# Moving one accumulator drain in four from VectorE to a ScalarE copy and an accumulating DMA

## What is computed

```python
h = linear_with_lora(x)                              # (8*128, 512)
q = dequant_matmul(h, qw_q, scales_q)                # 32 heads of 128
k, v = dequant_matmul(h, qw_k, scales_k), dequant_matmul(h, qw_v, scales_v)   # 8 heads of 128
ctx = softmax(mask(rope(q) @ rope(k).T / sqrt(128))) @ v
x = x + dequant_matmul(ctx, qw_o, scales_o)          # scales_o: one row of 512 for each head
x = x + ffn(low_rank(x))
```

## Time and profile before

| | |
|---|---|
| median of 3 runs | 567.71 us (567.18 to 568.55) |
| span of the profiled execution | 567.4 us (its own time isn't given apart from the span) |
| TensorE, matmuls | 544.6 us busy, 3183 instructions |
| VectorE | 485.5 us, 627 |
| ScalarE | 362.8 us, 939 |
| GpSimd | 400.2 us, 410 |
| DMA | 51.93 MB, mean 92 GB/s |

### The profile page before, as it was taken

How to read it: one execution, slowest core, us unless ns; L and a number is a source line. 1 busy time by engine, 2 the same in 40 slices (tenths; PEclk the granted TensorE clock), 3 DMA queues, 4 the chain that set the end, 5 groups by cost and what they waited for, 6 DMA issues and landing times.

```text
span 567.4 us, 10591 instructions
## 1 busy us (share of the span) xinstructions
PE 544.6 (96%) x3183; PEld 431.7 (76%) x3187; DVE 485.5 (86%) x627; ACT 362.8 (64%) x939; POOL 400.2 (71%) x410
## 2 busy tenths in 40 slices
PE   8999989999999999999999999999999999987985
PEld 6654778878888888888888888888888888864432
DVE  2753859998999899979997999799979998976997
ACT  2574476656665766576657665766576657556795
POOL 3005677799679977997799779977997799761053
PEclk9999999999999999999999999999999999999899
DMA  8932526412541254125422542154224312200003
GB/s 297 230 85 56 153 70 168 112 43 63 156 103 49 60 160 99 51 59 153 104 54 55 149 110 55 55 141 118 52 59 129 92 43 69 57 0 2 0 20 129
DMA packets 38173, 51.93 MB, mean 92 GB/s; under 512 B 12101, under 2 KB 20453, under 8 KB 38149
## 3 DMA queue, kind: packets, MB, share of 16 engines
q1 hardware_dynamic: 35652, 46.94, 31.5%
q10 hardware_dynamic: 2016, 3.48, 2.0%
q0 software_dynamic: 480, 1.22, 0.7%
HBM read 28.55 MB, written 2.10 MB: 54 GB/s over the span
## 4 chain that ended last, share of the span: by engine, by line
PE 82%; DVE 9%; issue 2%; ACT 2%; POOL 2%; DMA 2%; SPq 0%; DVEq 0%; ACTq 0%; POOLq 0%
PE pair L1389 23%; PE pair L1390 23%; PE flow L1378 9%; PE flow L1506 9%; PE flow L1498 4%; PE pair L1307 2%; DVE raw_v L1072 1%; PE flow L1383 1%; PE pair L1324 1%; PE flow L1307 1%; DVE y_max L1182 1%; DMA swap_q<-raw_q 1%; DVE ctx_lo L1093 1%; DVE probs L1194 1%; DVE rope_c L1194 1%
## 5 line engine op out<-in xcount | busy, mean ns | idle before, releaser
L1086 DVE SCALAR_TENSOR_TENSOR accT<-pair,so_now,accT 128x1024 f32<-128x1024 f32 x125 | 157.3, 1275 | 13.7 <-PE pair L1390 12.9
L1072 DVE SCALAR_TENSOR_TENSOR raw_q<-pair,sc_now,raw_q 128x1024 f32<-128x1024 f32 x90 | 115.4, 1283 | 6.3 <-ACT raw_q L769 2.9
L562 POOL TENSOR_TENSOR probs<-probs,rowinv 128x512 f32<-128x512 f32 x64 | 66.7, 1043 | 64.7 <-DVE rowinv L1059 64.6
L714 ACT ACTIVATE probs<-flow,negmax 128x128 f32<-128x128 f32 x248 | 87.6, 368 | 32.8 <-DVE negmax L1040 32.8
L1389 PE MATMUL pair<-ctx_hi,wo 128*128 128x512 f32 x256 | 104.9, 410 | 2.7 <-issue 1.5
L1390 PE MATMUL pair<-ctx_lo,wo 128*128 128x512 f32 x256 | 100.3, 392 | 0.0
L1389 PE MATMUL pair<-h_hi,wq 128*128 128x512 f32 x240 | 99.9, 416 | 0.0
L1390 PE MATMUL pair<-h_lo,wq 128*128 128x512 f32 x240 | 94.1, 392 | 0.0
L531 POOL TENSOR_TENSOR rope_s<-swap_q,consts 128x512 f32<-128x512 f32 x62 | 80.2, 1293 | 9.9 <-DMA swap_q<-raw_q 9.9
L543 POOL TENSOR_TENSOR qT<-rope_c,rope_s 128x512 f32<-128x512 f32 x62 | 79.4, 1280 | 4.4
L531 POOL TENSOR_TENSOR rope_c<-raw_q,consts 128x512 f32<-128x512 f32 x62 | 78.8, 1294 | 0.0
(11 more groups left out here) (243 smaller groups left out, 977.7 us busy)
## 6 DMA issues: line engine op xcount, KB each, us to landing
swap_q<-raw_q SPq DMA_DIRECT2D x62, 256.0 KB, 3.7
wq_i<-in_L_attn_qw_q SPq DMA_DIRECT2D x8, 1024.0 KB, 5.9
wo_i<-in_L_attn_qw_o SPq DMA_DIRECT2D x32, 256.0 KB, 2.7
swap_k<-raw_k SPq DMA_DIRECT2D x14, 256.0 KB, 3.6
wkv_i<-in_L_attn_qw_k SPq DMA_DIRECT2D x8, 256.0 KB, 3.6
wkv_i<-in_L_attn_qw_v SPq DMA_DIRECT2D x8, 256.0 KB, 4.0
stage<-in_x ACTq DMA_DIRECT2D x4, 256.0 KB, 4.8
probs<-in_L_ffn_w ACTq DMA_DIRECT2D x4, 256.0 KB, 7.2
```

Of the source, the lines that this page charges most:

```text
L562: pool.tensor_tensor(pr, pr, rowinv[:, f, :].unsqueeze(2).broadcast_to([P, HB, P]), ALU.mult).then_inc(probs_done, 1)
L714: e = act.activation(probs[:, 0, f, seq(b)], bank[:, seq(b)], ACT.Exp, bias=negmax[:, f, b:b + 1], accum_out=rowsum[:, f, b:b + 1])
L1072: dve.scalar_tensor_tensor(out=into, in0=flat(pair[pair_of(h, (kind, j), last, first)][:, :, :]), scalar=sc_now[:, scale_slot(kind, h), j: ...
L1086: dve.scalar_tensor_tensor(out=a, in0=flat(pair[pair_of(h, (O, c), last, first)][:, :, :]), scalar=so_now[:, (h if c == 0 else h - 1) % 2, ...
```

## The change

In heads 0, 1 and 2 of every group, head 0 of the first and head 2 of the last group excepted, step (O, 3) is no longer drained by VectorE. ScalarE copies the pair into a new tile `part_out` [128, 1024], times the scale (`part_output`, at the end of the head). GpSimd issues, in the next head, right behind the copy of `so_now`, a DMA that adds `part_out` onto `accT[:, 3, :]` (`add_part`). There is one `part_out`, so ScalarE's copy waits until the DMA before has landed (semaphore `d_added`). VectorE's next drain of chunk 3 (head 3 of a group, head 2 of the last one) waits for the DMA instead of for its own drain before. The waits that counted drains are recomputed: a pair that held such a step is free when ScalarE has copied it.

```diff
+        part_out = sb("part_out", [P, T])
...
+        d_added, part_made = sem("d_added"), sem("part_made")
...
+        ADDED_BY_DMA = (O, 3)
...
+        def added_by_dma(h, s, last):
+
+            return s == ADDED_BY_DMA and h % REP < REP - 1 and not (last and h >= 2)
+
+        def by_act(h, s, last):
+            return s[0] != O and s[1] == 0 or added_by_dma(h, s, last)
+
+        def dma_adds(g, h):
+
+            return (REP - 1) * g + h
...
+                    def add_part(late):
+
+                        _, c = ADDED_BY_DMA
+                        if not added_by_dma(late, (O, c), last and late >= 0) or first and late <= 0:
+                            return
+                        pool.dma_start(accT[:, c, :], part_out[:, :], accum_op=ALU.add).then_inc(d_added, 16)
...
-                            pool.wait_ge(dve_drained, drains_by(g, h - 1, (O, 3), first, last))
+                            pool.wait_ge(dve_drained, drains_by(g, h - 1, (O, 2), first, last))
+                            if added_by_dma(h - 1, (O, 3), last and h >= 1):
+                                pool.wait_ge(act_drained, drains_by(g, h - 1, (O, 3), first, last))
+                                wait(pool, d_added, 16 * (dma_adds(g, h - 1) - 1))
+                            if h == 1 or not added_by_dma(h - 1, (O, 3), last and h >= 1):
+                                pool.wait_ge(dve_drained, drains_by(g, h - 1 if h != 1 else -1, (O, 3), first, last))
                         pool.tensor_copy(so_now[:, h % 2:h % 2 + 1, :], so_cols[:, bass.ds(n, 1), :]).then_inc(so_set, 1)
+                        add_part(h - 1)
...
+                    def part_output():
+
+                        _, c = ADDED_BY_DMA
+                        if not present(h, (O, c), first, last) or not added_by_dma(h, (O, c), last):
+                            return
+                        act.wait_ge(step_done, steps_by(g, h, (O, c), first, last))
+                        wait(act, d_added, 16 * (dma_adds(g, h) - 1))
+                        wait(act, so_set, n)
+                        act.activation(part_out[:, :], flat(pair[pair_of(h, (O, c), last, first)][:, :, :]), ACT.Copy,
+                                       scale=so_now[:, (h - 1) % 2, c:c + 1]).then_inc(act_drained, 1)
...
                     seed_mask(1)
+                    part_output()
...
-                        if not present(h, (O, c), first, last):
+                        if not present(h, (O, c), first, last) or added_by_dma(h, (O, c), last):
                             return
...
-                        if not (first and (h == 0 or h == 1 and c > 0)):
+                        if added_by_dma(h - 1, (O, c), last and h > 0):
+                            dve.wait_ge(d_added, 16 * dma_adds(g, h - 1))
+                        elif not (first and (h == 0 or h == 1 and c > 0)):
                             dve.wait_ge(dve_drained, drains_by(g, h - 1, (O, c), first, last))
...
-                            pe.wait_ge(dve_drained, drains_by(g, 1, (O, 3), first, last))
+                            pe.wait_ge(act_drained, drains_by(g, 1, (O, 3), first, last))
```

More of the change, by code:

```diff
@@ L242, in present @@
             return not (last and (s[0] in (K, V) or s[0] == Q and h >= 2))
-        def by_act(s):
-            return s[0] != O and s[1] == 0
+        def added_by_dma(h, s, last):
[4 more added lines that the diff above has]
+            return (REP - 1) * g + h
         def pair_of(h, s, last=False, first=False):
@@ L254, in pair_of @@
             return at % 3 if at < len(STEPS) - 1 else 1
-        ACT_GROUP = sum(by_act(s) for _, s in STEPS)
+        ACT_GROUP = sum(by_act(h, s, False) for h, s in STEPS)
         DVE_GROUP = len(STEPS) - ACT_GROUP
@@ L266, in drains_by @@
         def drains_by(g, h, s, first, last):
-            act = by_act(s)
+            act = by_act(h, s, last and h >= 0)
+            skipped = sum(by_act(0, (O, c), False) == act for c in range(1, C))
+            group = ACT_GROUP if act else DVE_GROUP
             if h < 0:
-                later = [t for t in PERIOD[h][PERIOD[h].index(s) + 1:] if by_act(t) == act]
-                return ACT_GROUP * g - len(later) if act else DVE_GROUP * g - (SKIPPED + len(later))
-            mine = [t for t in STEPS if present(*t, first, last) and by_act(t[1]) == act]
+                later = [t for t in PERIOD[h][PERIOD[h].index(s) + 1:] if by_act(h, t, False) == act]
+                return group * g - (skipped + len(later))
+            mine = [t for t in STEPS if present(*t, first, last) and by_act(*t, last) == act]
             done = mine.index((h, s)) + 1
@@ L275, in drains_by @@
                 return done
-            return ACT_GROUP * g + done if act else DVE_GROUP * g + (done - SKIPPED)
+            return group * g + (done - skipped)
         def before_on_pair(h, s, first, last):
@@ L1462, in free_pair @@
                         if before is not None:
-                            drained = act_drained if by_act(before[1]) else dve_drained
+                            drained = act_drained if by_act(*before, last and before[0] >= 0) else dve_drained
                             pe.wait_ge(drained, drains_by(g, *before, first, last))
@@ L1580, in _ @@
                 here = [t for t in STEPS if present(*t, False, True) and pair_of(*t, True) == TAIL_PAIR[c]]
-                pe.wait_ge(dve_drained, drains_by(NKV - 1, *[t for t in here if not by_act(t[1])][-1], False, True))
+                pe.wait_ge(dve_drained, drains_by(NKV - 1, *[t for t in here if not by_act(*t, True)][-1], False, True))
                 slot = (NH - 1) % 2
```

## The result

The changed kernel takes **579.49 us** (median of 4 runs, 577.46 to 579.66), the kernel before 568.13 on the same chip (4 runs, 567.18 to 568.95): ratio 1.019, 95% interval 1.0166 to 1.0213, 11.4 us slower. The prediction said 572.5, in a range of 568.5 to 580. The direction and the range held, but the loss is more than twice the +4.8 forecast.

The account below looks back on a forecast made before the run. The prediction took TensorE as the bound, with VectorE costing it only 3.4 us. GpSimd's issues (+2.75 us) and the last group's wait for the DMA landing (+2.1) made +4.85 on 567.71: 572.5 us, range 568.5 to 580.

Parts of the forecast that it names:

- What bounds the kernel: Whole program: TensorE is the bound, every new wait costs its full length; VectorE directly costs it only 3.4 us.
- the first term: 22 DMA issues on GpSimd's queue, c = 0.7 us each, delay normalisations TensorE waits for: +2.75 us.
- VectorE's relief: 22 drains, 28 us, leave VectorE; the total gains only part of 3.4 us, 0.6 us in the last group.
- ScalarE's copies: 22 copies of 1.12 us at the end of a head fill ScalarE's idle time before the exponentials: cost nothing.
- the second term: Last group, head 2: VectorE's early drain waits for the DMA landing, D = 5.2; loss D - 3.1, +2.1 us.
- A slow DMA (1): D over 6.7 us, ScalarE's copy waits in heads 1 and 2, 13 times: 581 to about 592 us; chance 0.16.
- The fast one (2): The DMA lands like a swap, D = 3.7 us: total 571.0 us; chance 0.15.
- Hidden issues (3): GpSimd's queue issues while its datapath computes, c at most 0.3, D at most 4: 567.7 to 568.9 us; chance 0.13.
- VectorE as the bound (4): TensorE's seven V waits and two drain waits go, at most 3.4 us faster: 564.3 us; chance 0.06.
- The sum: Whole kernel: 2.75 + 2.1 = 4.85 us added to the median 567.71, said as 572.5 us.

Follow-up runs that it names:

- e5: The kernel before plus accumulating DMAs into a tile nobody reads, in head 1 of groups 1 to 7 and one ahead of the loop: 569.63 us, ratio 1.002.
- e6: The kernel before plus accumulating DMAs into a tile nobody reads, in head 2 of every group alone: 575.65 us, ratio 1.0136.
- e7: The kernel before plus accumulating DMAs into a tile nobody reads, in head 3 of groups 0 to 6 alone: 574.27 us, ratio 1.0101.
- e9: The changed kernel with a second `raw_q` tile taken by turns, so the Q drain waits for cosines of two heads back: 572.55 us, ratio 1.0068.
- e2: The changed kernel without its DMA and the waits for it, 22 output chunks never added: 566.79 us, ratio 0.9968 to the kernel before.
- e3: The changed kernel, but in the last group chunk 3 goes by DMA only in head 0: 576.21 us, ratio 1.0129 to the kernel before.
- e1: The kernel before plus 22 accumulating DMAs of 512 KB into a tile nobody reads, at the change's places: 579.71 us, ratio 1.019.
- e8: The kernel before plus 22 accumulating DMAs of only 16 KB into a tile nobody reads, at the change's places: 579.35 us, ratio 1.0205.
- e4: The changed kernel with the scales' copy and the DMA issue moved between the two normalisations: 566.94 us, ratio 0.9972 to the kernel before.

## Why the prediction was right and where it failed

**What bounds the kernel: right in its core, incomplete.** TensorE is the bound: its new waits of some 1.2 us per looped group are the group's 1.15. But between head 2 and head 0 GpSimd runs with at most a few tenths to spare, and the prediction looked for its margins only where TensorE waits for it directly.

**Issue on GpSimd's queue, the first term: the step that failed.** The cost c was taken as 0.7 and is 0.86. Had only this been off, the term would be 0.61 for each of the six groups instead of 0.45. The sentence that failed is "These delays don't add up, for each earlier stall moves TensorE away from the later one: the sum per group is the largest, c - 0.25". It costed the way over the first normalisations and the K addition, and took the 0.74 us of idle time before the second normalisation of head 3 as room to recover. It overlooked a third reader of GpSimd's position: cosines end, Q drain starts. The trace of before had it in plain sight, in GpSimd's and ScalarE's timelines of heads 3 and 0:

```profile
283.59 2.56 POOL L531 TENSOR_TENSOR rope_c<-raw_q,consts 128x512 f32<-128x512 f32 x2
...
298.35 2.53 POOL L531 TENSOR_TENSOR rope_c<-raw_q,consts 128x512 f32<-128x512 f32 x2
...
286.35 1.12 ACT L769 ACTIVATE raw_q<-pair,sc_now 128x1024 f32<-128x1024 f32 x1 [0.59 <-PE pair L1390]
...
301.07 1.12 ACT L769 ACTIVATE raw_q<-pair,sc_now 128x1024 f32<-128x1024 f32 x1 [1.03 <-PE pair L1390]
```

The cosines end at 286.15 and the drain starts at 286.35; in head 0 they end at 300.88 and it starts at 301.07. In the trace after, where this wait is named, the gaps are 290.71 to 290.90 and 306.30 to 306.49: the same 0.19. So the Q drain had no margin before either, though the view put its idle time down to TensorE's step, which came last by a hair. Through it GpSimd's lag reaches the second exponentials, the inverse and its own second normalisation, the idle time moves along with the lag, and the two issues add up: 0.65 + 0.82 per group instead of 0.45. The seventh group, for which the prediction had c - 0.65 = 0.05, loses 0.59 on the way to the last group's head 0 (16.24 for 15.65). e5 to e7 show the adding, e9 shows the way.

**VectorE's relief: undersized.** "What it gives the total ... is a part of the 3.4 us" looked for the gain in TensorE's waits for VectorE. It lay behind ScalarE: the maxima come sooner, the exponentials and with them the first normalisation of head 2, by 0.23 on the way to head 2 (e2). The prediction had seen "0.2 us earlier" and counted it as nothing. The V waits in head 3 did not stay as they were either, 4.0 us for 2.2, since the Q drains before them were late; in e9, where these aren't, the V waits are gone from the list.

**ScalarE's copies: right.** 22 copies of 1.11 us, never waiting for the DMA; no cost of them shows (e2).

**Landing time, the second term: right in kind and nearly in size, in part by luck.** D was taken as 5.2 and is 4.4 (4.54 to VectorE's start). The work behind it was put at 6.3 us and is 10.83 - 4.54 = 6.29. With D = 4.54 the formula gives 1.4; measured are 2.0 from head 2 to 3 (e3). The 0.6 between them is the gain that the prediction subtracted, with an issue that much sooner. It didn't come: the scales' copy ahead of the issue starts 1.24 us behind head 2's second inverse before (500.64, 499.40) and after (508.75, 507.51). VectorE's relief gives the last group 0.3 elsewhere (e2), so that its way from head 0 to 3 is 1.7 longer. Besides, the prediction put the cost of this issue itself at nothing, and e1 shows 0.84 for it where nobody waits for the landing; here the longer wait covers it. So a D too large by 0.7 and a gain too large by 0.6 nearly cancelled.

The Trainium skill's fit ("DMA: Bandwidth & Descriptors", Anatomy of one DMA: 2.0 us and bytes over 436 GB/s) gave an estimated 3.2 us; by its fixed part the trace of e8 agrees (2.1 us for 16 KB), by its rate it doesn't: 496 KB more take 2.3 us more, 221 GB/s, half of it, for an accumulating transfer. (The section doesn't say that its fit is for plain transfers; that was the prediction's reading. The two sizes differ in the length of their rows too.)

**The rivals.** A slow DMA (1) is out: ScalarE's copy never waited. The fast one (2) too, at 4.4. Hidden issues (3) are out: 0.86 behind both normalisations. The 0.2 in e4 isn't that rival, since GpSimd would have idled there. VectorE as the bound (4) is out as the sign of the whole, though its relief is worth 1.4 us.

**The sum.** Term one should have been (0.65 + 0.82 - 0.25 - 0.08) x 7 = 8.0, term two 1.7: 9.7, where the first loads show 9.5 and the medians 11.4.

## What to carry to other kernels

Before adding an operation to an engine's queue, list everybody who waits for anything behind it, also through tiles that get overwritten, and compare end and start times there: a wait that is nearly tied with another can stand under the other one's name. Idle time behind the new operation absorbs its delay only if what the engine waits for there does not itself depend on that engine's earlier work. Then look for idle time a few instructions away: here the same DMA was a loss of 2% behind two normalisations, and a gain of 0.3% between them.

## What the runs showed of the hardware

- A DMA issued by GpSimd stands in its queue for 0.86 us, whether it moves 512 KB or 16 KB (e1, e8). The next operation's record starts 0.59 us after the issue's start, and the three behind it read 1.59 us instead of 1.28; the lag in all is 0.86. The two issues at the start of the kernel before, 0.53 each, were no measure for it.
- An accumulating DMA of 512 KB within SBUF lands after 4.4 us (4.4 to 5.4), one of 16 KB after 2.1.
- No cost of the bytes themselves showed: the DMA share of a looped group rose from 0.35 to 0.48, and 22 x 512 KB cost the same as 22 x 16 KB (+11.6 and +11.0 us by the medians).
